# A first row whose norm is split in two, and a last row whose output is started early, in an attention and sparse-FFN kernel

## The reference

```python
xn = layernorm(x)                      # eps 1e-5
q, k, v = heads(xn @ Wq.T + bq), heads(xn @ Wk.T + bk), heads(xn @ Wv.T + bv)   # 16 heads of 16
q, k = rope(q), rope(k)
att = softmax(where(causal, q @ k.T / 4, -inf))
attn = (att @ v) merged @ Wo.T + bo
prob = softmax(xn @ router_w.T + router_b)          # 16 blocks
mask = the 4 blocks of 16 with the highest prob
h = relu(where(mask, xn @ w1.T + b1, 0))            # 1024 hidden, 16 blocks of 64
ffn = h @ w2.T + b2
out = x + attn + ffn
```

## Time and profile before

| what | value |
|---|---|
| median of 3 runs (lowest to highest) | 874.66 us (874.31 to 875.78) |
| the profiled execution's own time | 870.45 us |
| its span, first to last instruction | 868.7 us |
| PE busy | 839.0 us, 97% of the span, 5440 instructions |
| DVE, ACT, POOL busy | 539.1, 457.3, 281.5 us |
| mean granted clock of TensorE | 0.996 |

### The profile page before, as it was taken

One profiled execution on the slowest core, in us unless ns is written; L12 is line 12 of the kernel. 1 busy time (PEld: TensorE's weight loads), 2 busy tenths in 40 slices (PEclk: granted clock), 3 DMA queues, 4 the chain that ended last, 5 costly groups with the idle time before them and its releaser, 6 DMA issues.

```text
span 868.7 us, 15130 instructions
## 1 busy us (share of the span) xinstructions
PE 839.0 (97%) x5440; PEld 504.5 (58%) x5440; DVE 539.1 (62%) x1727; ACT 457.3 (53%) x1065; POOL 281.5 (32%) x298
## 2 busy tenths in 40 slices
PE   3899999999999999999999999999999999999996
PEld 2576454554556555656656656555656656565664
DVE  5948966666976657565775656657566665656201
ACT  2512455665656555455565554646465654646563
POOL 4366045726540069060640018524420002000000
PEclk9999999999999999999999999999999999999999
DMA  8672305231403053231410234140250314000001
GB/s 288 219 206 99 75 3 141 97 107 61 131 32 75 26 169 100 75 75 48 114 63 9 67 99 141 43 111 2 75 148 2 75 60 113 2 3 1 3 1 49
DMA packets 45626, 69.65 MB, mean 80 GB/s; under 512 B 5104, under 2 KB 20336, under 8 KB 45552
## 3 DMA queue, kind: packets, MB, share of 16 engines
q1 hardware_dynamic: 45552, 68.69, 26.8%
HBM read 38.93 MB, written 29.75 MB: 79 GB/s over the span
## 4 chain that ended last, share of the span: by engine, by line
PE 89%; DVE 5%; DMA 2%; ACT 1%; SPq 1%; issue 1%; POOL 0%; ACTq 0%; DVEq 0%; POOLq 0%
PE o_bank L1002 15%; PE banks L986 15%; PE banks L936 14%; PE banks L924 13%; PE banks L911 12%; PE banks L885 5%; PE banks L973 3%; PE banks L989 3%; PE banks L894 3%; PE banks L951 2%; PE banks L915 1%; DMA k_st<-term_scratch 1%; DVE banks L1205 1%; DVE part_max L1202 1%; PE banks L875 1%; PE banks L961 1%
## 5 line engine op out<-in xcount | busy, mean ns | idle before, releaser
L804 ACT ACTIVATE probs<-banks 128x512 f32<-128x512 f32 (+3 forms) x768 | 337.2, 498 | 256.8 <-PE banks L989 185.3
L986 PE MATMUL banks<-q_st,k_st 99*128 99x512 bf16 (+3 forms) x768 | 241.2, 327 | 1.2 <-DVE row_max L1205 0.7
L936 PE MATMUL banks<-k_st,q_st 96*128 96x512 bf16 (+3 forms) x768 | 238.0, 327 | 2.5 <-DMA k_st<-term_scratch 1.6
L1202 DVE TENSOR_REDUCE part_max<-banks 128x1 f32<-128x512 f32 x256 | 160.8, 683 | 49.9 <-PE banks L936 49.3
L1205 DVE CUSTOM_DVE_ANT_0 banks<-banks,tri,part_max 128x512 f32<-128x512 f32 (+3 forms) x256 | 131.6, 555 | 82.5 <-PE banks L936 81.8
L1205 DVE CUSTOM_DVE_ANT_0 banks<-banks,tri 128x512 f32<-128x512 f32 (+3 forms) x256 | 121.5, 513 | 80.5 <-PE banks L936 79.8
L1002 PE MATMUL o_bank<-probs,v_sb 128*17 128x512 f32 (+3 forms) x1536 | 142.7, 489 | 0.1
L664 POOL TENSOR_SCALAR max_neg<-row_max 128x16 f32<-128x16 f32 x32 | 8.1, 254 | 407.7 <-DVE row_max L1205 407.7
L911 PE MATMUL banks<-xnT,w_sb 128*128 128x256 f32 x512 | 137.3, 391 | 0.2 <-ACT probs L804 0.2
L936 PEld LDWEIGHTS banks<-k_st,q_st 96*128 96x128 bf16 x768 | 73.9, 98 | 87.3 <-issue 31.7
L924 PE MATMUL banks<-w_sb,hT 128*128 128x256 f32 x512 | 121.3, 383 | 0.3 <-DVE row_max L1205 0.3
(11 more groups left out here) (80 smaller groups left out, 749.4 us busy)
## 6 DMA issues: line engine op xcount, KB each, us to landing
term_scratch<-pieces SPq DMA_DIRECT2D x96, 256.0 KB
q_st<-term_scratch SPq DMA_DIRECT2D x16, 768.0 KB, 5.8
k_st<-term_scratch SPq DMA_DIRECT2D x16, 768.0 KB, 8.4
acc<-in_x SPq DMA_DIRECT2D x8, 512.0 KB, 4.0
out<-acc SPq DMA_DIRECT2D x8, 512.0 KB, 2.9
x_sb<-in_x SPq DMA_DIRECT2D x3, 1024.0 KB, 6.5
x_sb<-in_x SPq DMA_DIRECT2D x2, 512.0 KB, 4.6
w_sb<-in_w1T SPq DMA_DIRECT2D x1, 1024.0 KB, 9.1
```

Of the source, the lines that this page charges most:

```text
L804: nc.scalar.activation(probs[:, u % P_SLOTS, h, 0:w], filled("score", n, k, h)[:, 0:w], ACT.Exp, scale=SCALE).then_inc(s_out, 1)
L936: nc.tensor.matmul(bank[:, 0:w], q_st[0:KROWS, at, h, i * P:(i + 1) * P], k_st[0:KROWS, at, h, c * HALF:c * HALF + w], start=True, stop=Tr ...
L986: last = nc.tensor.matmul(bank[:, 0:w], k_st[0:SROWS, at, h, j * P:(j + 1) * P], q_st[0:SROWS, at, h, q0:q0 + w], start=True, stop=not dia ...
L1202: ins = nc.vector.tensor_reduce(part_max[:, h, at:at + 1], bank[:, 0:w], AX.X, ALU.max)
```

## The change

The norm of the first row is taken in two halves of four tiles each, with x arriving in four DMAs of two tiles. The Newton steps are three instead of four, in all rows. TensorE runs 18 transposes of the identity (`WARM`) as soon as it has landed, ahead of its first real work. ScalarE runs one exponential on a small tile (`warm`) early. `FIRST` projects the first half of the tokens before the second half of x is turned, and takes in two FFN tiles at its end (`ffn(0, 0, 1)`). GpSimd waits for `unsel_ready` instead of `first_low` before it adds the biases to acc. In the last row y's first half is turned, and multiplied by Wo, within the last group; the second half is normalised, turned (`yTl`), multiplied, added and stored in two parts of two tiles. The planner's list starts with `begun = False`, under which no maximum is put between the parts of an FFN tile.

```diff
-NEWTON = 4
-LN_STEPS = 2 * NT + 3 + 3 * NEWTON
+NEWTON = 3
+LN_CHAIN = 3 + 3 * NEWTON
+LN_STEPS = 2 * NT + LN_CHAIN
+WARM = 18
...
-FIRST = (xnT_of(0, 0, 1, 2, 3) + proj(0, (0, 0), (0, 1), (1, 0), (1, 1)) + values_of(0, *range(NT))
-         + proj(0, (2, 0), (2, 1), (3, 0), (3, 1)) + [("unselT", 0)] + hid(0, 0, *range(FB)))
+FIRST = (xnT_of(0, 0, 1) + proj(0, (0, 0), (1, 0)) + xnT_of(0, 2, 3) + proj(0, (0, 1), (1, 1))
+         + values_of(0, *range(NT)) + proj(0, (2, 0), (2, 1), (3, 0), (3, 1)) + [("unselT", 0)]
+         + hid(0, 0, *range(FB)) + ffn(0, 0, 1))
...
-            w += after(0, ffn(b, 3) + hid(b, 2, *range(FB)) + ffn(b, 4))
+            w += after(0, hid(b, 2, *range(FB)) + ffn(b, 4))
...
             w += after(0, hid(b, 3, *range(FB)) + ffn(b, 6, 7))
+            if not more:
+                w += after(8, yT_of(b, 0, 1)) + after(9, out_of(b, 0, 1))
...
-            if maxed < len(maxima) and may_fill("max"):
+            if begun and maxed < len(maxima) and may_fill("max"):
...
-    works = ffn(0, 0, 1) + hid(0, 1, *range(FB)) + ffn(0, 2)
+    works = hid(0, 1, *range(FB)) + ffn(0, 2, 3)
...
-LAST = ([("oT", GROUPS - 1, 1)] + yT_of(B - 1) + out_of(B - 1, 0, 1, 2, 3))
+LAST = ["run", ("oT", GROUPS - 1, 1), ("yTl", 0), ("yTl", 1)] + out_of(B - 1, 2, 3)
...
-            for h in range(2):
-                t = slice(h * NT // 2, (h + 1) * NT // 2)
-                sp.dma_start(x_sb[:, t, :], x_rows[0][:, t, :]).then_inc((x_half_in, x_in)[h], 16)
+            for u in range(NT // 2):
+                t = slice(2 * u, 2 * u + 2)
+                sp.dma_start(x_sb[:, t, :], x_rows[0][:, t, :]).then_inc((*x_pair_in, x_in)[u], 16)
...
-            for h in range(2):
-                store_out(B - 1, h)
+            store_out(B - 1, 0)
+            for u in range(2, 4):
+                sp.wait_ge(m_out, M_COUNT["out", B - 1, u])
+                t = slice(2 * u, 2 * u + 2)
+                sp.dma_start(out_rows[B - 1, :, t, :], acc[:, t, :]).then_inc(stored[1], 16)
...
-            pool.wait_ge(first_low, 4)
+            pool.wait_ge(unsel_ready, 1)
...
+            def take_last_yT(part):
+                bank = filled("yTl", part)
+                t = slice(HALF + part * QTR, HALF + (part + 1) * QTR)
+                for kb in range(KB):
+                    last = nc.scalar.activation(yT[:, kb, t], bank[:, kb * QTR:(kb + 1) * QTR], ACT.Identity,
+                                                bias=bv_sb[:, kb:kb + 1])
+                last.then_inc(s_out, 1)
...
+            act.wait_ge(pad_set, 1)
+            nc.scalar.activation(warm[:, 1:2], warm[:, 0:1], ACT.Exp)
             act.wait_ge(bqk_in, 32)
...
             pe.wait_ge(ident_in, 16)
+            for _ in range(WARM):
+                nc.tensor.transpose(banks[:, BANKS - 1, 0:P], ident[:], ident[:])
...
-            ln_stats(0, *range(NT))
+            nc.vector.memset(warm[:], 0.0).then_inc(pad_set, 1)
             nc.vector.memset(logits[:], LOWEST).then_inc(pad_set, 1)
             nc.vector.memset(top4[:], LOWEST).then_inc(pad_set, 1)
-            ln_factors()
-            ln_apply(*range(NT))
             nc.vector.memset(o_bank[:], 0.0).then_inc(pad_set, 1)
+            for first in (0, NT // 2):
+                tiles = range(first, first + NT // 2)
+                ln_stats(0, *tiles)
+                ln_factors(first, first + NT // 2)
+                ln_apply(*tiles)
...
             turn_halves(0, 3)
+            add_ffn(0, 0)
+            add_ffn(0, 1)
```

149 lines of the change are left out of this document (95 added, 54 removed).

## The result

| | before | after |
|---|---|---|
| median (lowest to highest), 6 runs each | 874.63 us (870.61 to 877.55) | 864.57 us (863.50 to 865.89) |
| ratio, 95% interval | | 0.9892 [0.9874, 0.9910] |
| profiled execution, its span | 870.45, 868.7 us | 864.99, 863.2 us |
| mean granted clock | 0.996 | 0.998 |

The change makes the kernel 10.1 us faster. The forecast was 872.7 with a range of 869.3 to 875.6: the direction was right, the size was not, and the result lies outside the range. The two profiled executions differ by 5.5 us; the other 4.6 lie between them and the medians. Of all runs in this document one, of e9_ffn_behind (966.29 us, granted clock 0.85), was in a slower state; it counts in no range or ratio here, and the median of 870.57 given there would be 870.41 without it.

A forecast was written before the change was run, and what follows sets the result against it. TensorE, busy 839.0 of 868.7 us, was taken as the bound. Head 0.8 plus tail 1.1 gave 1.9 off 870.45, so 868.5; with the median's 4.2 carried over, 872.7, range 869.3 to 875.6.

The forecast's parts named there:

- Routing, hidden units, FFN tiles: Head: routing's transposes from 41.94 to 40.1, hidden units done at 51.3, two FFN tiles, first maximum at 58.3, 3.5 later.
- The stacked operands: Loaded inputs of the first maximum: expected between 52.7 and 55.5, in every case before 58.3.
- D: Rival: operands come later than 58.3, every us counts fully, 873.7 at 59.3; 13% together with C.
- What VectorE makes of it: Maxima after the head: they begin 3.5 later, the 64th only 1.9 later; head's gain 0.8, bounds -3 to 3.5.
- 3.3 - 0.6: Head: 3.3 us of TensorE work done earlier, less 0.6 because the 78th maximum is issued in the 77th's place.
- 3.8 - L: Whole change's gain in us, from 3.3 - 0.6 + 1.1 - L; a loss of 0.2% from L = 5.5 on.
- L: Lateness of the 64th maximum against the kernel before; the sum gave 1.9 us.
- The tail: Last `pv` to end: 16.8 becomes 10.5, 6.3 less; minus 3.6, 0.9 and 0.7 moved ahead, gain 1.1 (0.2 to 1.9).
- The start: Norm, warming and first projections: warming until 10.9, first projection at 12.6, second half's rope 1.8 earlier (0.8 to 2.8).
- A: Rival: VectorE does not decide, all of 3.5 stays with 1.1 of the tail, 870.1; 27%.
- B: Rival, slower: TensorE waits ahead of the turned maxima, VectorE stands still, L grows; 876.9 at 6.0; 10%.
- C: Rival: the dropped Newton links were hidden in gaps between maxima, L stays 3.5, 874.4; 13% together with D.

The follow-up runs named there:

- e9_ffn_behind: The changed kernel with FFN tiles 0 and 1 behind the first maxima instead of ahead of them; 870.57 us, ratio 0.9963.
- e2: The changed kernel with GpSimd waiting for first_low again before it adds the biases; 868.62 us, ratio 0.9941.
- e1: The kernel before with one edit, GpSimd waiting for unsel_ready before it adds the biases; 874.99 us, ratio 1.0010.
- e11: The kernel before with only GpSimd's new wait and the two FFN tiles ahead of the first maximum (`begun` with it); 868.86 us, ratio 0.9932.
- e10: The changed kernel with the identity's DMA issued ahead of x and 36 warming transposes instead of 18; 865.41 us, ratio 0.9894.
- e14: The kernel before with 18 dummy transposes of the identity ahead of the first maximum only; 872.34 us, ratio 0.9983.
- e3: The changed kernel without the warming transposes (WARM = 0); 866.65 us, ratio 0.9913.
- e6: The changed kernel with the identity's DMA issued ahead of x; 864.56 us (four runs), ratio 0.9885.
- e15: e10 with three hidden blocks of the next tokens moved ahead of the first maximum; 863.09 us (five runs), ratio 0.9867.
- e16: The changed kernel with one hidden block of the next tokens moved ahead of the first maximum; 865.37 us, ratio 0.9891.

## Why the prediction was wrong

The forecast missed by 8.1 us. Of these, 3.5 lie in the profiled execution (868.5 forecast, 864.99 measured), and there the error is one step of the sum; the other 4.6 lie in how a profile's difference was carried over to the median, and that part stays open.

**The step that failed** is "Routing, hidden units, FFN tiles". It said that the routing's transposes move to 40.1, that "a like idle time remains, and with it the low clock", and hence a first maximum at 58.3. The change of GpSimd's wait stood in the diff; the step asked only whether the biases would be ready in time, not what they had been running beside. They had held VectorE for 2.9 us. With them out of the way TensorE idles for 1.21 us instead of 3.53, its clock does not fall, and the stretch from the routing's transposes to the end of the hidden units takes 8.4 us instead of 11.2. The first maximum came 4.4 us before its forecast. e2 (+4.05 with the old wait) shows what it is worth; e1 (both instructions short again, no gain alone) and e11 (5.1 us together with the FFN tiles) show what it needs.

**The stacked operands** were forecast to come between 52.7 and 55.5 and came at 53.9. That term was right, but it was taken as no bound, since TensorE was to arrive at 58.3. In truth TensorE arrived at 53.3, and the landing set the first maximum. D, "the operands are late", was dismissed for the same reason; it describes e1, e9, e10 and e14.

**What VectorE makes of it** came out right in size, in part by luck. From the first maximum to the second splitting 36.2 were forecast and 36.1 measured, to the third 44.1 and 43.9. But the 1.6 us between the 48th and the 64th maximum were argued from a guess and four Newton steps standing there, of which 8 links would go. The trace of before has only the guess and one step there; the three other steps begin at 104.47, behind the third splitting.

```profile
93.92 0.15 DVE L1102 TENSOR_SCALAR guess<-var 128x8 int32<-128x8 int32 x1
...
94.87 0.57 DVE L1205 CUSTOM_DVE_ANT_0 banks<-banks,tri 128x384 f32<-128x384 f32 x1 [0.59 <-PE banks L936]
```

The stretch fell from 9.61 to 7.82. All five of its links left it, about 1.0, and VectorE's waits for TensorE in it fell from 1.16 (0.59 and 0.57) to 0.35. e11, with four Newton steps, has the same 7.83: it is the order, not the dropped step.

The work that the new order takes out of the rest was counted as 3.3 - 0.6 = 2.7; the traces give 751.4 - 748.7 = 2.7. With "3.8 - L" and the measured L of -2.7 the formula gives 6.5, against 7.0 (5.50 + 1.46) by the profiles without the low stretch at 220 us.

**The tail** was under-sized by 0.5: the 0.7 us charged for ScalarE's two copies did not appear (the wait for them is 0.32), and the saving was 6.1 instead of 6.3. By medians it is 2.7, which six runs each can't tell from 1.6.

**The start** was right in mechanism: warming until 10.9, the first 8 transposes behind it in 1.40, where the 16 of before took 3.65. It was counted only through the 1.8 us of the rope, which the operands' landing then swallowed. What it also does is to keep the first projection from being slow: 1.95 or 1.96 us in all seven profiles in which the warming ran up to x, 3.75 without it (e3) and where it ended 2.45 us too early (e6).

**Carrying over to the median** cost 4.6 us. The profile of before stood 4.2 us under its median; the forecast assumed that the change leaves this distance. It fell to about 1 (864.57 against 863.5, the profile of after without its low stretch). Shown is that lateness of the operands and low clock at a few places can make up such a distance, and that e15, in which TensorE does not wait for the operands, scatters by 0.2 us. The recorded clocks say that the runs of before above 875 had more low clock than its profile or as much, but not where, and no run of before above 872 was profiled. Which of these losses a run at 874.6 had stays open.

**Rivals.** A (870.1) was nearest, but not by its mechanism, which keeps a head's gain of 3.5 behind a first maximum at 58.3: VectorE was let in earlier instead. B and C did not happen.

## What to carry to other kernels

When an edit delays work on GpSimd, look in the trace at what VectorE did while that work ran, and compare the same instructions elsewhere: here a 128x32 copy of 2.35 us was the sign. Time won ahead of a DMA's landing is worth nothing by itself, and may let the clock fall; it becomes a gain when work from behind the landing is put there (e11, e15), as long as the new order doesn't make VectorE wait elsewhere (e16). Cut the trace at marks that both kernels share (here first maximum, third splitting, last `pv`), so that a forecast can be checked stretch by stretch, and do not carry one execution's distance from the median over to a kernel whose waits differ.
